# Two moves inside the step of a Mamba-style mixer: where TensorE makes the state products, and which of two VectorE updates goes first

## The chip, the cores and the metric

The kernel runs on one core of one Trainium2 chip. Time is device microseconds (us) of one execution. Five engines run their own instruction lists side by side and meet only at semaphores: TensorE (PE in the profile, its weight loads PEld), VectorE (DVE), ScalarE (ACT), GpSimd (POOL) and SyncE (SP), which here only issues DMA transfers.

## The reference: what is computed

Two batches of 512 tokens, 512 features. Four residual blocks: a block-sparse linear layer, a feed-forward block with 4-bit style dequantised weights, a state-space mixer (Mamba-2 form), and the same feed-forward block again. The change lies in the mixer:

```python
gate, hBC, dt = split(norm(x) @ in_proj_w.T)          # 8192 gate, 8192 x + 2*1024 B,C, 128 dt
x, Bm, Cm = split(silu(causal_conv4(hBC)))            # 128 heads of 64; B, C: 8 groups of 128
M       = (C B^T) * exp(segment_sum(A dt))            # per chunk of 128 tokens: "decayed group product"
Y_diag  = M @ (x dt)                                  # inside a chunk
states  = B_decay^T @ (x dt)                          # what a chunk adds to the state
new     = carry of the states over the chunks         # s[c] = exp(A_last) s[c-1] + states[c]
Y_off   = C @ s * exp(A_cumsum)                       # from earlier chunks
y = rmsnorm(Y_diag + Y_off + D x) * norm_w * silu(gate)
out = y @ out_proj_w.T                                # 8192 -> 512
```

## The kernel before

The mixer is written out as 128 steps `k` (K), each for one batch and one pair of heads (128 channels, all 512 tokens of that batch, 4 chunks of 128), plus five steps that drain it. Each engine has its own order, written by hand, in a loop `for k in range(STEPS)`. There is no planner: the order in the file is the order in each engine's queue.

In step k **TensorE** does: `project` of the x unit k+1 (12 matmuls of 512 columns, L847), `outputs(k-1)` (Y_diag and Y_off of the pair before, L910 and L916), `arguments(k)` (the decay exponents, L873), `turn_x(k)` (four transposes, L885), in every eighth step `gram` (C B^T and B transposed, L857 and L863), `project` of the z (gate) unit k+1, `states(k)` (six small products, L896), in two of eight steps `project` of a b or c unit for the next group, and `project_out`, one tile of the output projection (12 matmuls, L929). The out tiles start at k = 5, the b and c units come at k = 3, 4, 11, 12, and so on, for the groups 1 to 15; gram comes in the step behind the c unit's. Below, these three are called the b step, the c step and the gram step, and the five others ordinary steps.

**VectorE** in step k: `y_low(k-2)` (L1252), `accumulate` of the out tile of step k-1 (L1262), `decay_c(k)` (L1225, the tile ce), the convolution of the x unit k+1 (three instructions, L1171), `scale_x(k)` (x_dec L1193, x_dt L1198), `mask_gram` (L1178) in a gram step, `gate(k-1)` (L1242, L1246), `carry(k)` (a copy L1207 and four small instructions L1213: the state over the chunks), `mask_em(k)` (L1233: the decayed group product em), and behind these the convolution of a b or c unit (L1171 with the tile bc).

**ScalarE** taps a projected bank (`tap`, L1037: first term of the convolution), copies weights (L1025, L1081), does the exponentials (L1063, L1065), `y_high` (L1075), `square` (L1069), the activations of x, z (L1042, L1047), the tap of b or c, and after the c unit's convolution `activate_bc` (L1052). **GpSimd** makes the low parts of the weights (L1350, L1355) and sums squares (L1365).

What ties them: every projected unit, gram, B transposed and out tile goes to one of three PSUM banks (`ring`) in turn, and `ring_free` waits for the reader of the bank three uses earlier. In a gram step the z unit takes the bank of the x unit k+1 of the same step, so it waits for that unit's convolution (`conv_done`). `states(k)` waits for x_dec (`xdec_done`); `carry(k)` for `states(k)` (`st_mm`); `outputs(k)` for em, x_dt, ce and the carried state (`em_done`, `xdt_done`, `ce_done`, `st_done`).

Of the kernel before, what the change touches and what calls it, by code (L numbers as in the profile page):

```python
# [37 lines left out]
K = B * JP  # L38
# [9 lines left out]
def build(nc, x_in, mask_t, wa_t, bias_a, w_in, conv_w, conv_b, dt_bias, a_log, d_res, norm_w, w_out,  # L48
          gu_w, gu_z, gu_s, dn_w, dn_z, dn_s, x_mid, e_t, a_parts, out):
    with ExitStack() as ctx:  # L50
# [644 lines left out]
        def need(eng, s, n):  # L695
            if n > 0:
                eng.wait_ge(s, n)
# [37 lines left out]
        def gram_in(k):  # L735

            if k < 0:
                return [0]
            n, q = k // QG + 1, k % QG
            return [n] if q == 5 and n < NG else []  # L740
# [14 lines left out]
        def ring_bank(banked):  # L755
            return RING[RINGED[banked] % 3]
# [15 lines left out]
        with nc.Block() as block:  # L772
# [52 lines left out]
            def _(pe):  # L825
                def ring_free(banked):
                    at = RINGED[banked] - 3
                    if at < 0:
                        return
                    kind, i = RING_AT[at]  # L830
                    if kind in ("x", "b", "c"):
                        pe.wait_ge(conv_done, CONVED[kind, i] + 1)
                    elif kind == "z":
                        pe.wait_ge(silu_z, i + 1)
                    elif kind == "gram":
                        pe.wait_ge(gt_done, i + 1)
                    elif kind == "btok":
                        pe.wait_ge(btok_done, i + 1)
                    else:
                        pe.wait_ge(acc_done, CPB * i[0] + i[1] + 1)  # L840

                def project(unit):
                    u, b, dst = UNIT[unit], unit_batch(unit), ring_bank(unit)
                    ring_free(unit)
                    pe.wait_ge(w_lo, u + 1)
                    for i, (k, (wp, xp)) in enumerate((k, ab) for k in range(KT) for ab in PASSES):
                        mm = nc.tensor.matmul(dst[:], w_sb[:, u % WR, wp, k * P:(k + 1) * P],  # L847
                                              lnt[:, xp, k, b * S:(b + 1) * S],
                                              start=(i == 0), stop=(i == 3 * KT - 1))
                    mm.then_inc(prj_mm, 1)  # L850
# [38 lines left out]
                def states(k):  # L889
                    pe.wait_ge(xdec_done, k + 1)  # L890
                    pe.wait_ge(btok_done, k // QG + 1)
                    if k == 0:
                        pe.wait_ge(last_done, B)
                    need(pe, st_done, k)
                    for c in range(OFFC):
                        mm = nc.tensor.matmul(ST[:, c * PAIR:(c + 1) * PAIR],  # L896
                                              b_tok[:, k // QG % 2, c * NS:(c + 1) * NS],
                                              x_dec[:, c * PAIR:(c + 1) * PAIR], start=True, stop=True)
                    mm.then_inc(st_mm, 1)

                def outputs(k):
                    pe.wait_ge(em_done, k + 1)
                    pe.wait_ge(xdt_done, k + 1)
                    pe.wait_ge(ce_done, k + 1)
                    pe.wait_ge(st_done, k + 1)
                    need(pe, y_done, k)
                    for c in range(CPB):
                        for h in range(2):
                            at = (2 * c + h) * HD
                            mm = nc.tensor.matmul(YT[h * HD:(h + 1) * HD, c * CS:(c + 1) * CS],  # L910
                                                  x_dt[:, at:at + HD], em[:, h, c * CS:(c + 1) * CS],
                                                  start=True, stop=(c == 0))
                        if c == 0:
                            continue
                        for h in range(2):
                            mm = nc.tensor.matmul(YT[h * HD:(h + 1) * HD, c * CS:(c + 1) * CS],  # L916
                                                  state[:, c - 1, h * HD:(h + 1) * HD],
                                                  ce[:, k % 2, h, (c - 1) * CS:c * CS],
                                                  start=False, stop=True)
                    mm.then_inc(yt_mm, 1)  # L920

                def project_out(i, t):
                    dst = ring_bank(("out", (i, t)))
                    ring_free(("out", (i, t)))
                    pe.wait_ge(yg_lo, HALF * (i + 1))
                    pe.wait_ge(wo_lo, HALF * (i + 1))
                    for m, (j, (yp, wp)) in enumerate((j, ab) for j in range(HALF * i, HALF * (i + 1))
                                                      for ab in PASSES):
                        mm = nc.tensor.matmul(dst[:], ygs[:, j % OR, yp, t * P:(t + 1) * P], wo[:, j % WOR, wp],  # L929
                                              start=(m == 0), stop=(m == 3 * HALF - 1))  # L930
                    mm.then_inc(out_mm, 1)
# [68 lines left out]
                for k in range(STEPS):  # L1000
                    if 0 < k < K - 1:
                        project(("x", k + 1))
                    if 1 <= k <= K:
                        outputs(k - 1)
                    if k < K:
                        arguments(k)
                        turn_x(k)
                    for n in gram_in(k):
                        gram(n)
                    if k + 1 < K:  # L1010
                        project(("z", k + 1))
                    if k < K:
                        states(k)
                    for unit in bc_units(k):
                        project(unit)
                    for i, t in out_tiles(k):
                        project_out(i, t)

            @block.scalar
            def _(act):  # L1020
# [139 lines left out]
            def _(dve):  # L1160
# [41 lines left out]
                def carry(k):  # L1202
                    dve.wait_ge(st_mm, k + 1)
                    if k == 0:
                        dve.wait_ge(last_done, B)
                    need(dve, yt_mm, k)
                    nc.vector.tensor_copy(state[:, 0], ST[:, 0:PAIR]).then_inc(st_part, 1)  # L1207
                    for c in range(1, OFFC):
                        dve.wait_ge(st_part, (2 * OFFC - 2) * k + 2 * c - 1)
                        for h in range(2):  # L1210
                            at = 2 * pair(k) + h
                            last = c == OFFC - 1 and h == 1
                            nc.vector.scalar_tensor_tensor(  # L1213
                                out=state[:, c, h * HD:(h + 1) * HD],
                                in0=state[:, c - 1, h * HD:(h + 1) * HD],
                                scalar=e_last[:, batch(k) * CPB + c, at:at + 1],
                                in1=ST[:, c * PAIR + h * HD:c * PAIR + (h + 1) * HD],
                                op0=ALU.mult, op1=ALU.add)\
                                .then_inc(st_done if last else st_part, 1)
# [9 lines left out]
                def mask_em(k):  # L1229
                    dve.wait_ge(exp_done, k + 1)  # L1230
                    dve.wait_ge(gt_done, k // QG + 1)
                    need(dve, yt_mm, k)
                    nc.vector.tensor_tensor(  # L1233
                        em[:], ARG[:],
                        gt[:, k // QG % 2].rearrange("p (o t) -> p o t", o=1).to_broadcast([P, 2, S]),
                        ALU.mult).then_inc(em_done, 1)
# [87 lines left out]
                for k in range(STEPS + 1):  # L1324
                    if 2 <= k <= K + 1:
                        y_low(k - 2)
                    for i, t in out_tiles(k - 1):
                        accumulate(i, t)
                    if k < K:
                        decay_c(k)  # L1330
                    if k + 1 < K:
                        conv(("x", k + 1))
                    if k < K:
                        scale_x(k)
                    for n in gram_in(k):
                        mask_gram(n)
                    if 1 <= k <= K:
                        gate(k - 1)
                    if k < K:
                        carry(k)  # L1340
                        mask_em(k)
                    for unit in bc_units(k):
                        conv(unit)

# [185 lines left out]
```

## Time and profile before

| | us |
|---|---|
| median of 3 runs (2245.4 to 2248.91) | 2247.79 |
| the profiled execution | 2245.92 |
| its span | 2244.2 |
| PE busy in the span | 2123.8 (95%) |
| DVE busy | 1645.7 (73%) |
| ACT busy | 1389.9 (62%) |
| POOL busy | 891.8 (40%) |

The mixer's steps run from about 355 to 1955 us of the span. In the timeline a row is a run of like instructions: start in us, length in us, engine, line, operation, tile written and tiles read, shape, count; in brackets the idle time of that engine before it and what ended the idle time. Starts are the numbers to go by: ends overlap the next row's start, because the engines are pipelined.

### The profile page before, as it was taken

What the parts mean: (1) busy time and instruction counts of PE and PEld (TensorE: products, weight loads), DVE (VectorE), ACT (ScalarE), POOL (GpSimd) and SP (SyncE); (2) the same over time, 40 slices, a digit from 0 to 9 for tenths busy, and PEclk for the clock granted to TensorE, in tenths of its full rate; (3) what the DMA queues carried; (4) which work ended last, traced back from release to release, by engine and by line L of the source; (5) the groups of instructions that cost most, each with busy time, mean ns of one, the idle gap of its engine ahead of it and who ended that gap; (6) DMA issues with size and microseconds to landing.
All of it is one profiled execution on the core that took longest, in us unless ns stands there. A gap on an engine that the chain in (4) does not pass through costs nothing. (4 is left out here: it accounts for less than half of the span.)

```text
span 2244.2 us, 37403 instructions
## 1 busy us (share of the span) xinstructions
PE 2123.8 (95%) x13374; PEld 1739.7 (78%) x13374; DVE 1645.7 (73%) x2683; ACT 1389.9 (62%) x1872; POOL 891.8 (40%) x637
## 2 busy tenths in 40 slices
PE   5999977899999999999999999999999999959999
PEld 4788865787887878787888888787887878748887
DVE  8655466778787787878787777778787877755554
ACT  2222236777777777777777777777787777622221
POOL 2222123454444445453444445454444444342221
PEclk9999988999999999999999999999999999979999
DMA  4434313333333333333333323333333333323441
GB/s 164 143 128 150 103 63 104 105 98 102 100 101 102 106 95 103 100 97 103 100 104 99 107 96 112 91 107 96 96 107 96 107 96 108 121 92 134 168 134 73
DMA packets 128564, 241.89 MB, mean 108 GB/s; under 512 B 13968, under 2 KB 48528, under 8 KB 128144
## 3 DMA queue, kind: packets, MB, share of 16 engines
q1 hardware_dynamic: 128400, 239.73, 33.3%
q8 instruction: 100, 1.64, 0.3%
q14 instruction: 64, 0.52, 0.1%
HBM read 234.17 MB, written 5.51 MB: 107 GB/s over the span
## 5 line engine op out<-in xcount | busy, mean ns | idle before, releaser
L847 PE MATMUL ring<-m_lnt,w_sb 128*128 128x512 f32 x3456 | 850.0, 395 | 17.7 <-DVE xc L1171 17.7
L847 PEld LDWEIGHTS ring<-m_lnt,w_sb 128*128 128x128 f32 x3456 | 638.6, 189 | 148.4 <-DVE xc L1171 21.4
L1350 POOL TENSOR_TENSOR w_sb<-w_raw,w_sb 128x512 fp32r<-128x512 f32 x288 | 420.0, 1463 | 338.2 <-ACT w_sb L1025 337.4
L1171 DVE SCALAR_TENSOR_TENSOR xc<-ring,cw,xc 128x511 f32<-128x511 f32 (+2 forms) x384 | 287.2, 748 | 183.8 <-ACT xc L1037 174.7
L929 PE MATMUL ring<-wo,ygs 128*128 128x512 f32 x1536 | 383.0, 398 | 2.5 <-POOL wo L1355 2.5
L1365 POOL TENSOR_TENSOR ysq<-ysq,y 128x512 f32<-128x512 f32 x126 | 163.6, 1298 | 542.9 <-ACT y L1069 542.9
L929 PEld LDWEIGHTS ring<-wo,ygs 128*128 128x128 f32 x1536 | 282.5, 189 | 60.6 <-issue 3.1
L1025 ACT ACTIVATE w_sb<-w_raw 128x512 fp32r<-128x512 f32 x288 | 177.4, 622 | 33.4 <-DMA w_raw<-w_in 33.3
L910 PE MATMUL yt<-em,x_dt 128*64 128x128 f32 x2048 | 183.6, 279 | 1.4 <-DVE em L1233 1.4
L1037 ACT ACTIVATE xc<-ring,cb,cw 128x512 f32<-128x512 f32 x128 | 99.2, 775 | 137.4 <-PE ring L847 137.4
L1063 ACT ACTIVATE arg<-arg 128x1024 f32<-128x1024 f32 x128 | 129.0, 1008 | 69.2 <-PE arg L873 69.2
L1355 POOL TENSOR_TENSOR wo<-wo_raw,wo 128x512 fp32r<-128x512 f32 x128 | 170.2, 1329 | 3.3 <-ACT wo L1081 3.3
L365 PE MATMUL bank_e<-f_lnt,f_gu 128*128 128x512 f32 x672 | 159.6, 399 | 11.2 <-DVE f_lnt L135 6.5
L288 POOL TENSOR_TENSOR f_gu<-f_gu_f,f_gu 128x1024 fp32r<-128x1024 f32 x28 | 67.2, 2401 | 251.1 <-ACT f_gu L312 251.1
L1065 ACT ACT_TABLE_LOAD x128 | 164.2, 1283 | 2.3
L1042 ACT ACT_TABLE_LOAD x127 | 162.9, 1283 | 2.3
L365 PEld LDWEIGHTS bank_e<-f_lnt,f_gu 128*128 128x128 f32 x672 | 129.9, 194 | 39.7 <-issue 10.6
L365 PE MATMUL bank<-f_lnt,f_gu 128*128 128x512 f32 x672 | 154.1, 390 | 3.5 <-DVE f_hf L251 1.8
L1233 DVE TENSOR_TENSOR em<-arg,gt 128x1024 f32<-128x1024 f32 x128 | 155.8, 1217 | 0.1
L910 PEld LDWEIGHTS yt<-em,x_dt 128*64 128x64 f32 x2048 | 118.0, 136 | 46.7 <-issue 43.3
L365 PEld LDWEIGHTS bank<-f_lnt,f_gu 128*128 128x128 f32 x672 | 125.9, 188 | 30.3 <-issue 4.1
L916 PE MATMUL yt<-ce,state 128*64 128x128 f32 x1536 | 149.1, 273 | 0.0
(176 smaller groups left out, 3081.4 us busy)
## 6 DMA issues: line engine op xcount, KB each, us to landing
w_raw<-w_in SPq DMA_DIRECT2D x288, 256.0 KB, 4.3
ce<-e_t SPq DMA_DIRECT2D x128, 384.0 KB, 4.2
wo_raw<-w_out SPq DMA_DIRECT2D x128, 256.0 KB, 4.5
f_gu_q<-gu_w SPq DMA_DIRECT2D x28, 512.0 KB, 5.2
f_gu_zr<-gu_z SPq DMA_DIRECT2D x28, 512.0 KB, 6.8
f_gu_sr<-gu_s SPq DMA_DIRECT2D x28, 512.0 KB, 8.0
f_dn_q<-dn_w SPq DMA_DIRECT2D x28, 256.0 KB, 7.1
f_dn_zr<-dn_z SPq DMA_DIRECT2D x28, 256.0 KB, 7.8
```

The lines of the kernel that those rows point to most:

```text
L365: mm = nc.tensor.matmul(dst[half][:], gu[:, j, b, c:c + P], lnt[:, a, k, half * TOK:(half + 1) * TOK], start=(i == 0), stop=(i == 3 * KT - 1))
L847: mm = nc.tensor.matmul(dst[:], w_sb[:, u % WR, wp, k * P:(k + 1) * P], lnt[:, xp, k, b * S:(b + 1) * S], start=(i == 0), stop=(i == 3 * K ...
L910: mm = nc.tensor.matmul(YT[h * HD:(h + 1) * HD, c * CS:(c + 1) * CS], x_dt[:, at:at + HD], em[:, h, c * CS:(c + 1) * CS], start=True, stop ...
L929: mm = nc.tensor.matmul(dst[:], ygs[:, j % OR, yp, t * P:(t + 1) * P], wo[:, j % WOR, wp], start=(m == 0), stop=(m == 3 * HALF - 1))
L1025: nc.scalar.activation(w_sb[:, u % WR, 0], w_raw[:, u % NR], ACT.Copy).then_inc(w_hi, 1)
L1042: nc.scalar.activation(xc[:, k % 3], xc[:, k % 3], ACT.Silu).then_inc(silu_x, 1)
L1065: nc.scalar.activation(part, part, ACT.Exp, scale=-1.0).then_inc(exp_done, 1)
L1171: nc.vector.scalar_tensor_tensor(out=dst[:, d:S], in0=src[:, 0:S - d], scalar=cw[:, tile, j:j + 1], in1=dst[:, d:S], op0=ALU.mult, op1=ALU ...
L1233: nc.vector.tensor_tensor(em[:], ARG[:], gt[:, k // QG % 2].rearrange("p (o t) -> p o t", o=1).to_broadcast([P, 2, S]), ALU.mult).then_inc ...
L1350: nc.gpsimd.tensor_tensor(w_sb[:, u % WR, 1], w_raw[:, u % NR], w_sb[:, u % WR, 0].bitcast(F32), ALU.subtract).then_inc(w_lo, 1)
L1355: nc.gpsimd.tensor_tensor(wo[:, j % WOR, 1], wo_raw[:, j % 2], wo[:, j % WOR, 0].bitcast(F32), ALU.subtract).then_inc(wo_lo, 1)
L1365: nc.gpsimd.tensor_tensor(part, part, y[:, k % 2], ALU.add).then_inc(ysq_done, 1)
```

## The change

On TensorE `states(k)` goes behind the b or c unit and the out tile, to the end of the step. On VectorE `mask_em(k)` goes ahead of `carry(k)`. Nothing is added or taken away.

```diff
--- before.py
+++ after.py
@@ -1009,12 +1009,12 @@
                         gram(n)
                     if k + 1 < K:
                         project(("z", k + 1))
-                    if k < K:
-                        states(k)
                     for unit in bc_units(k):
                         project(unit)
                     for i, t in out_tiles(k):
                         project_out(i, t)
+                    if k < K:
+                        states(k)
 
             @block.scalar
             def _(act):
@@ -1337,8 +1337,8 @@
                     if 1 <= k <= K:
                         gate(k - 1)
                     if k < K:
+                        mask_em(k)
                         carry(k)
-                        mask_em(k)
                     for unit in bc_units(k):
                         conv(unit)
```

## Rows read from the trace of the kernel before

**Rows 1.** The page, part 1: busy time of each engine in the span.
```profile
PE 2123.8 (95%) x13374; PEld 1739.7 (78%) x13374; DVE 1645.7 (73%) x2683; ACT 1389.9 (62%) x1872; POOL 891.8 (40%) x637
```

**Rows 2.** Waits, 350 to 1900 us: total us, times, longest.
```profile
DVE state L1207 <- PE st L896: 47.9, 106, 4.3
...
PE ring L847 <- DVE xc L1171: 17.7, 16, 3.4
...
PE st L896 <- DVE x_dec L1193: 15.6, 14, 3.6
```

**Rows 3.** Timeline of PE, an ordinary step: states, out tile, next x unit.
```profile
1041.57 0.83 PE L896 MATMUL st<-x_dec,b_tok 128*128 128x128 f32 x6
1042.15 3.02 PE L929 MATMUL ring<-wo,ygs 128*128 128x512 f32 x12
1045.01 2.88 PE L847 MATMUL ring<-m_lnt,w_sb 128*128 128x512 f32 x12
```

**Rows 4.** Timeline of DVE, the same step.
```profile
1042.43 0.29 DVE L1207 COPY state<-st 128x128 f32<-128x128 f32 x1 [0.37 <-PE st L896]
...
1043.66 1.22 DVE L1233 TENSOR_TENSOR em<-arg,gt 128x1024 f32<-128x1024 f32 x1
...
1048.74 2.31 DVE L1171 SCALAR_TENSOR_TENSOR xc<-ring,cw,xc 128x511 f32<-128x511 f32 x3 [1.80 <-ACT xc L1037]
```

**Rows 5.** Timeline of PE, from the x unit ahead of a c step to the gram step.
```profile
1004.23 2.88 PE L847 MATMUL ring<-m_lnt,w_sb 128*128 128x512 f32 x12
...
1013.38 0.94 PE L896 MATMUL st<-x_dec,b_tok 128*128 128x128 f32 x6 [0.94 <-DVE x_dec L1193]
...
1019.63 2.88 PE L847 MATMUL ring<-m_lnt,w_sb 128*128 128x512 f32 x12
...
1027.20 3.03 PE L847 MATMUL ring<-m_lnt,w_sb 128*128 128x512 f32 x12 [0.88 <-DVE xc L1171]
```

**Rows 6.** Timeline of DVE, the same stretch.
```profile
1004.50 2.32 DVE L1171 SCALAR_TENSOR_TENSOR bc<-ring,cw,bc 128x511 f32<-128x511 f32 x3 [3.13 <-ACT bc L1037]
...
1008.75 1.88 DVE L1225 TENSOR_TENSOR ce<-ce,bc 128x768 f32<-128x768 f32 x1
1010.55 2.31 DVE L1171 SCALAR_TENSOR_TENSOR xc<-ring,cw,xc 128x511 f32<-128x511 f32 x3
...
1019.68 2.31 DVE L1171 SCALAR_TENSOR_TENSOR bc<-ring,cw,bc 128x511 f32<-128x511 f32 x3 [1.97 <-ACT bc L1037]
```

**Rows 7.** Timeline of ACT, the same stretch.
```profile
1018.88 0.77 ACT L1037 ACTIVATE bc<-ring,cb,cw 128x512 f32<-128x512 f32 x1
1022.03 1.06 ACT L1052 ACTIVATE bc<-bc 128x1024 f32<-128x1024 f32 x1 [2.38 <-DVE bc L1171]
```

**Rows 8.** Timeline of POOL, the same stretch.
```profile
1008.54 1.27 POOL L1350 TENSOR_TENSOR w_sb<-w_raw,w_sb 128x512 fp32r<-128x512 f32 x1 [0.86 <-ACT w_sb L1025]
```

**Rows 9.** Timeline of PE, two groups later: a c step without a wait.
```profile
1206.12 2.88 PE L847 MATMUL ring<-m_lnt,w_sb 128*128 128x512 f32 x12
...
1220.33 2.88 PE L847 MATMUL ring<-m_lnt,w_sb 128*128 128x512 f32 x12
...
1227.86 3.02 PE L847 MATMUL ring<-m_lnt,w_sb 128*128 128x512 f32 x12 [0.84 <-DVE xc L1171]
```

**Rows 10.** Timeline of PE, steps 126 and 127, with no x unit between.
```profile
1938.81 0.83 PE L896 MATMUL st<-x_dec,b_tok 128*128 128x128 f32 x6
1939.39 3.02 PE L929 MATMUL ring<-wo,ygs 128*128 128x512 f32 x12
1942.34 0.66 PE L910 MATMUL yt<-em,x_dt 128*64 128x128 f32 x8
```

**Rows 11.** Timeline of PE at two idle times of over 2 us.
```profile
326.48 0.65 PE L955 MATMUL xt<-ident,dt_h 128*128 128x128 f32 x4 [2.28 <-DVE dt_h L1297]
...
1957.27 12.75 PE L929 MATMUL ring<-wo,ygs 128*128 128x512 f32 x48 [2.54 <-POOL wo L1355]
```

**Rows 12.** Windows behind those: length, busy PE to POOL, granted PEclk, DMA, GB/s.
```profile
326.40:327.50 1.10, 1.02 (x9) 1.03 (x10) 0.35 (x2) 0.00 (x0) 0.00 (x0) 1.00 0.01 2
...
1957.20:1958.00 0.80, 0.73 (x2) 0.66 (x3) 0.00 (x0) 0.00 (x0) 0.00 (x0) 0.53 0.63 241
```

## The prediction

> **What bounds the kernel now.** I read the busy line first: TensorE is busy for 95% of the span and VectorE for 73% [rows 1]. So the question is only where TensorE idles in the mixer, and whether the change touches it. The list of waits answers that for 350 to 1900 us: 15.6 us in 14 waits of the state products for x_dec, and 17.7 us in 16 waits of a projection for the convolution xc [rows 2]. All of TensorE's other time there is matmuls. The 47.9 us that VectorE waits for the state products [rows 2] are idle time of an engine that is not the bound.
>
> The timeline then says where the two waits stand. In an ordinary step there is none: states, out tile and next x unit follow each other [rows 3]. They come once per group of eight steps: 0.94 us ahead of states in the c step, 0.88 us ahead of the z unit in the gram step [rows 5]. Both have one source, a chain VectorE -> ScalarE -> VectorE through these three steps: the convolution of the b unit (1004.50), ce (1008.75), the convolution of the x unit (1010.55), x_dec and the gate behind it [rows 6], ScalarE's tap of the c unit (1018.88), the convolution of the c unit (1019.68), ScalarE's activation of B and C (1022.03) [rows 6, 7] and, after it in ScalarE's queue, the tap of the next x unit, that unit's convolution, and then the z unit at 1027.20 [rows 5]. The most the change can win is the first wait, about 15 us in all, if the second does not grow by as much.
>
> **TensorE, ordinary steps.** The same work in another order: z, out, states, x instead of z, states, out, x. States take 1042.15 - 1041.57 = 0.58 us, the out tile 1045.01 - 1042.15 = 2.86 us [rows 3]; the sum stays. States now start 0.58 us ahead of the next x unit, here at 1044.43. The carry can start 1042.43 - 1041.57 = 0.86 us after states start [rows 3, 4] and frees VectorE 1043.66 - 1042.43 = 1.23 us later [rows 4], so 2.09 us after states start: 1046.52. `outputs` needs the carried state behind the x unit, at 1045.01 + 2.8 = 1047.8. It is ready 1.3 us early. No wait, cost nothing; the cover is the x unit.
>
> **VectorE, ordinary steps.** em moves ahead, into the time in which VectorE now waits for states. The carry ends at 1046.52. Behind it are queued y_low, accumulate and ce, which take about 2.15 us (they filled the time from the end of em, about 1044.8, to the start of the 1.80 us wait, 1046.94 [rows 4]). 1046.52 + 2.15 = 1048.67, and the next convolution started at 1048.74, waiting for its tap [rows 4]. It just fits. The 0.37 and 1.80 us of idle time per step become one wait of about 2.2 us in front of the carry.
>
> What may be late next is ce. One row shows ce at 1.88 us, started at 1008.75 while GpSimd's subtraction ran from 1008.54 to 1009.81 [rows 6, 8]; VectorE went on only 0.74 us after GpSimd had ended. In ordinary steps ce and y_low now fall 1.7 us later, onto GpSimd's two subtractions. So the convolution may be late by up to one such hold, about 1.3 us, in some steps. I price this at nothing, as it is absorbed by the 2.2 us wait in front of the carry of the same step. Bounds: nothing, and (if two holds come together) 2.6 - 2.2 = 0.4 us in each of some 75 ordinary steps, 30 us. I take nothing, since the row shows one hold.
>
> The Trainium skill, page "SBUF — State Buffer", in its part on the port pair that VectorE and GpSimd share, has the rule: an exclusive lock, and a VectorE operation with two SBUF inputs is blocked for the whole of a GpSimd instruction that started first, and the other way round. The trace agrees (1.88 us beside 1.27 us of GpSimd). By that rule a VectorE instruction can be held anew by each GpSimd instruction, and both y_low and ce have two SBUF inputs; this is the rule that speaks against the change, and the rival on holds below is its result.
>
> **The b, c and gram steps.** Count from the x unit that stands ahead of the c step, T0 = 1004.23 [rows 5].
> - b step: states now come at T0 - 0.58, the carry frees VectorE at T0 + 1.51 = 1005.74. The convolution of the b unit, queued behind the carry, started at 1004.50: 1.24 us later. But then y_low, at about 1007.98, falls into GpSimd's idle time (0.86 us up to 1008.54 [rows 8]) and is not held, and ce meets the same instruction of GpSimd (1008.54 to 1009.81, which follows TensorE, not VectorE) and ends where it did: the x convolution stays at 1010.55. Cost nothing, cover: the time ce was held anyway. If that cover is gone, up to 1.24 us.
> - c step: the wait of 0.94 us goes, since states now stand 5.5 us later, far behind x_dec. A c step without the wait is in the trace: from x unit to x unit 1220.33 - 1206.12 = 14.21 us [rows 9], against 1019.63 - 1004.23 = 15.40 [rows 5]. TensorE gets 1.19 us ahead.
> - what is late next: the convolution of the c unit is queued behind the carry. States start at T0 + 14.21 - 0.58 = T0 + 13.63, VectorE is free at T0 + 13.63 + 2.09 = T0 + 15.72. Before, this convolution started at 1019.68 = T0 + 15.45, released by ScalarE's tap. So the moved states set it, 0.27 us later than before.
> - gram step: from that convolution to the z unit the chain has no slack: 1027.20 - 1019.68 = 7.52 us [rows 5, 6]. The z unit comes at T0 + 15.72 + 7.52 = T0 + 23.24, against T0 + 22.97 before. TensorE, 1.19 us ahead, waits 0.88 + 1.19 + 0.27 = 2.34 us there. The saved wait is handed back whole, with 0.27 us on top.
>
> Fifteen groups have these steps. In twelve the rows are as above: 12 x 0.27 = 3.2 us. In two (z unit at 1227.86 and about 100 us later) TensorE had no wait in the c step, because the chain ran faster: from T0 to z 1227.86 - 1206.12 = 21.74 us [rows 9]. There the carry is the new limit, and z comes at T0 + 23.24: 2 x 1.50 = 3.0 us. In the first group ScalarE's chain sets both ends, and I take nothing.
>
> **The end.** In steps 126 to 127 no x unit follows. outputs(126) started 2.95 us after the out tile [rows 10]. Now the out tile starts at 1938.81, states about 2.8 us later at 1941.6, the carry is done at 1941.6 + 2.09 = 1943.7, and outputs(126) starts then instead of at 1942.34: 1.4 us. In step 127 the same happens again, with VectorE already late by it; together 1.5 us, between 1.0 and 2.0. Nothing hides this: the tail waits for outputs(127).
>
> **Sum.** 3.2 + 3.0 + 1.5 = 7.7 us. On the profiled execution: 2245.9 + 7.7 = 2253.6 us. That execution lies 1.9 us under the median of the runs, 2247.8, so for a median I forecast 2247.8 + 7.7, about 2255 us (+0.3%). Changes under 0.2%, 4.5 us, can't be told from none.
>
> **Rivals.**
> - **The clock falls.** Behind an idle time of 2.28 us the granted clock was 1.00; behind one of 2.54 us it was 0.53, half speed (1.2 instead of 2.4 GHz) [rows 11, 12]. The new wait in the gram step, 2.34 us, lies between. Where it fell, 48 matmuls took 12.75 us [rows 11]; four runs of 12 take 4 x 2.73 = 10.9 in full clock (a run of 12 behind another), so it costs 1.8 us a time. In all 14 groups 26 us: 2281 us; in half of them 2268 us. For it: 2.34 is over the longest idle time that is shown harmless. Against: by 0.06 us only. Chance 0.2.
> - **Holds make VectorE the bound** in ordinary steps: y_low and ce both held, 2.6 us against 2.2 us of wait, up to 30 us, 2285 us at most. Against: VectorE's idle time hardly runs out with one hold. Chance 0.04.
> - **Faster: the first wait goes and the second does not take it.** Place: the c step. It would decide if the convolution of the c unit started at least 0.5 us earlier than T0 + 15.45, that is, if carry and tap were both early: then 0.94 us of 12 to 14 groups stay won, less the end's 1.5 us: -11 us, 2237 us. For it: the two short groups, where that chain is 1.23 us shorter. Against: carry needs states, and states stand at T0 + 13.63 by TensorE's own pace. Chance 0.10.
> - **Nothing to be seen:** the 0.27 us is not there (the carry comes in time) and only the two short groups and the end cost: 3 to 4.5 us, 2251 us. Chance 0.16.
>
> **Numbers.** Forecast 0.50. In a fifth of it the result falls under 4.5 us. Slower: 0.40 + 0.20 + 0.04 = 0.64. Same: 0.10 + 0.16 = 0.26. Faster: 0.10. The range goes from 2247 (the null case with the scatter of the runs, 3.5 us) to 2272 (the clock lost in more than half of the groups).
>
> **What would show it.** In the waits: states for x_dec gone; the projection's wait for xc up from 17.7 us to about 35 us in 16 waits of 2.2 to 2.4 us; VectorE's wait for st up from 48 us to over 200 us, and its wait for the tap of xc nearly gone. In the timeline: the convolution of the c unit directly behind the carry, not behind a tap; T0 to z in the gram step 23.2 us in all fifteen groups but the first; outputs(126) behind a wait for the carry (or st). Wrong if T0 to z is under 22.9 us, if waits for the state appear ahead of outputs in ordinary steps, or if the granted clock is under 1 behind the gram step.

## The result, and the profile after

| | before | changed |
|---|---|---|
| median, 6 runs each, us | 2246.86 (2244.93 to 2248.91) | 2254.89 (2253.13 to 2259.19) |
| profiled execution, us | 2245.92 | 2253.62 |
| its span, us | 2244.2 | 2251.9 |

The ratio is 1.004, 95% interval 1.0027 to 1.0052: slower by about 8 us, clear of the 0.2% that can be told.

The waits in the same window as [rows 2] (engine and line, who was waited for, total us, times, longest):

```profile
DVE state L1207 <- PE st L896: 229.5, 118, 4.2
...
PE ring L847 <- DVE xc L1171: 26.4, 16, 3.4
...
PE ring L847 <- ACT sz L1047: 6.7, 14, 0.5
...
PE yt L910 <- DVE state L1213: 2.3, 3, 0.9
...
PE st L896 <- DVE x_dec L1193: 1.2, 1, 1.2
```

TensorE's wait for x_dec has all but gone (15.6 to 1.2 us), its wait for xc has grown (17.7 to 26.4 us), and a new one is there, 14 times about 0.5 us: an x unit waits for ScalarE's activation of z to free its bank. VectorE's wait for the products has grown from 47.9 to 229.5 us, and costs nothing by itself.

TensorE, from the x unit ahead of a c step to the gram step, the stretch of [rows 5]:

```profile
1006.07 0.83 PE L896 MATMUL st<-x_dec,b_tok 128*128 128x128 f32 x6
1006.66 3.02 PE L847 MATMUL ring<-m_lnt,w_sb 128*128 128x512 f32 x12
...
1020.29 0.83 PE L896 MATMUL st<-x_dec,b_tok 128*128 128x128 f32 x6
1021.58 3.06 PE L847 MATMUL ring<-m_lnt,w_sb 128*128 128x512 f32 x12 [0.46 <-ACT sz L1047]
...
1029.89 3.04 PE L847 MATMUL ring<-m_lnt,w_sb 128*128 128x512 f32 x12 [1.44 <-DVE xc L1171]
```

VectorE in the same stretch, against [rows 6]:

```profile
1011.59 1.59 DVE L1225 TENSOR_TENSOR ce<-ce,bc 128x768 f32<-128x768 f32 x1
1013.10 2.31 DVE L1171 SCALAR_TENSOR_TENSOR xc<-ring,cw,xc 128x511 f32<-128x511 f32 x3
...
1021.15 0.29 DVE L1207 COPY state<-st 128x128 f32<-128x128 f32 x1 [2.11 <-PE st L896]
1021.48 0.98 DVE L1213 SCALAR_TENSOR_TENSOR state<-state,e_last,st 128x64 f32<-128x64 f32 x4
1022.38 2.31 DVE L1171 SCALAR_TENSOR_TENSOR bc<-ring,cw,bc 128x511 f32<-128x511 f32 x3
```

The convolution of the c unit starts directly behind the carry, at T0 + 15.72 (1022.38 - 1006.66), and z in the gram step at T0 + 23.23 (1029.89 - 1006.66).

Where the 7.7 us of span came from, by the starts of TensorE's landmarks: from the z unit of the first gram step to that of the second 100.94 us before, 102.98 after (+2.04); the 13 further intervals to the last gram step 1309.98 before, 1314.01 after (+4.03: before, 11 of about 100.96 and 2 of about 99.72 us; after, all of about 101.08); from there to the square sums 138.58 before, 140.51 after (+1.93); the rest -0.3. In the first group TensorE waits twice, 2.51 us ahead of gram and 2.57 us ahead of the z unit, and runs the z unit at half clock. Its rows, and three windows (length, busy PE to POOL, PEclk, DMA, GB/s):

```profile
417.47 1.16 PE L857 MATMUL ring<-bc 128*128 128x128 f32 x8 [2.51 <-ACT bc L1052]
...
421.53 4.93 PE L847 MATMUL ring<-m_lnt,w_sb 128*128 128x512 f32 x12 [2.57 <-DVE xc L1171]
```
```profile
418.00:418.80 0.80, 0.80 (x9) 0.72 (x7) 0.00 (x0) 0.80 (x2) 0.79 (x1) 1.00 0.01 5
418.90:419.00 0.10, 0.06 (x1) 0.00 (x0) 0.00 (x0) 0.10 (x1) 0.10 (x1) 0.50 0.00 0
421.50:423.00 1.50, 1.47 (x4) 1.20 (x5) 1.50 (x3) 1.49 (x3) 0.23 (x1) 0.50 0.04 11
```

The clock is at 0.50 already at 418.90 us, ahead of the second wait (421.53 - 2.57 = 418.96): it fell behind the first, the wait of gram for ScalarE's activation. The kernel before has no such wait there. Its z unit, behind a wait of 2.05 us, runs at full clock, and the next row starts 2.88 us later; here that is 4.76 us.

### The profile page after: what moved, and what is told of

The parts are those of the page before. It is cut to its first block and busy times, and to the rows that moved or that the text cites. A ratio compares the mean times of both kernels' runs of the same rounds, so it can differ in the third digit from the quotient of the medians.

```text
span 2251.9 us, 37403 instructions
## 1 busy us (share of the span) xinstructions
PE 2127.8 (94%) x13374; PEld 1745.5 (78%) x13374; DVE 1680.3 (75%) x2683; ACT 1389.9 (62%) x1872; POOL 926.3 (41%) x637
## 5 line engine op out<-in xcount | busy, mean ns | idle before, releaser
L847 PE MATMUL ring<-m_lnt,w_sb 128*128 128x512 f32 x3456 | 860.0, 399 | 33.1 <-DVE xc L1171 26.4
L1350 POOL TENSOR_TENSOR w_sb<-w_raw,w_sb 128x512 fp32r<-128x512 f32 x288 | 410.9, 1431 | 335.7 <-ACT w_sb L1025 335.3
L929 PE MATMUL ring<-wo,ygs 128*128 128x512 f32 x1536 | 369.0, 389 | 2.4 <-POOL wo L1355 2.4
L929 PEld LDWEIGHTS ring<-wo,ygs 128*128 128x128 f32 x1536 | 288.3, 188 | 62.8 <-issue 3.1
L1355 POOL TENSOR_TENSOR wo<-wo_raw,wo 128x512 fp32r<-128x512 f32 x128 | 215.7, 1685 | 3.3 <-ACT wo L1081 3.3
L1207 DVE COPY state<-st 128x128 f32<-128x128 f32 x128 | 37.3, 292 | 238.3 <-PE st L896 238.3
L1225 DVE TENSOR_TENSOR ce<-ce,bc 128x768 f32<-128x768 f32 x128 | 183.8, 1436 | 0.0
L1075 ACT ACTIVATE ygs<-sz 128x512 fp32r<-128x512 f32 x128 | 80.9, 632 | 128.4 <-DVE sz L1246 128.4
```

The costliest lines, as they stand in the source:

```text
L1225: nc.vector.tensor_tensor(ce[:, k % 2], ce[:, k % 2], c_off.rearrange("p (o t) -> p o t", o=1) .to_broadcast([P, 2, OFFC * CS]), ALU.mult) ...
L1350: nc.gpsimd.tensor_tensor(w_sb[:, u % WR, 1], w_raw[:, u % NR], w_sb[:, u % WR, 0].bitcast(F32), ALU.subtract).then_inc(w_lo, 1)
L1355: nc.gpsimd.tensor_tensor(wo[:, j % WOR, 1], wo_raw[:, j % 2], wo[:, j % WOR, 0].bitcast(F32), ALU.subtract).then_inc(wo_lo, 1)
```

## The experiments

My theory was the prediction's: the loss is the carry, which waits for products that TensorE makes at T0 + 13.6 us, and which stands ahead of the c unit's convolution in VectorE's queue. The rivals: VectorE's new order by itself; the holds between VectorE and GpSimd; TensorE's order by itself. Medians are of 4 to 8 runs; each ratio is against the kernel before on the same chip.

### One half at a time

Only em ahead of the carry:

```diff
-                        carry(k)
                         mask_em(k)
+                        carry(k)
```

> Only VectorE's half of the change: em ahead of the carry, the state products where they were. Theory (the loss comes from the carry standing behind state products that come at T0 + 13.6 us): no change, 2244 to 2249 us, T0 to z of the gram step still 22.97 us, because the products come early and em and carry fill the same time in either order. Rival (the loss comes from VectorE's own new order, em ahead of the carry): slower by most of the 8 us, 2252 us or more.

Measured: 2233.57 us, ratio 0.9945 (0.9932 to 0.9959). Neither: 12 to 14 us **faster**. Half of the change was a gain, and I had priced it at nothing. The reason is in the c step. VectorE and GpSimd of this kernel:

```profile
1001.91 0.67 DVE L1262 TENSOR_TENSOR xr<-xr,ring 128x512 f32<-128x512 f32 x1
1002.51 0.95 DVE L1225 TENSOR_TENSOR ce<-ce,bc 128x768 f32<-128x768 f32 x1
1003.38 2.30 DVE L1171 SCALAR_TENSOR_TENSOR xc<-ring,cw,xc 128x511 f32<-128x511 f32 x3
```
```profile
1002.65 1.96 POOL L1350 TENSOR_TENSOR w_sb<-w_raw,w_sb 128x512 fp32r<-128x512 f32 x1 [1.21 <-ACT w_sb L1025]
```

ce starts at 1002.51, 0.14 us ahead of GpSimd's subtraction. It takes 0.95 us and GpSimd is held (1.96 us); before, GpSimd came first and ce took 1.88 us [rows 6, 8]. So these two engines meet not only at semaphores. TensorE of the same kernel:

```profile
998.35 2.88 PE L847 MATMUL ring<-m_lnt,w_sb 128*128 128x512 f32 x12
...
1012.56 2.88 PE L847 MATMUL ring<-m_lnt,w_sb 128*128 128x512 f32 x12
...
1020.02 3.02 PE L847 MATMUL ring<-m_lnt,w_sb 128*128 128x512 f32 x12 [0.77 <-DVE xc L1171]
```

T0 to z is 21.67 us, not 22.97: this group now looks like the two short ones of before [rows 9]. The traces show that the start order decides it. In the kernel before, ce starts 0.05 and 0.07 us ahead of GpSimd in the two short groups, and 0.03 to 0.21 us behind it in the twelve others. With em first it is ahead by 0.02 to 0.22 us in 13 of 14 groups; in the one where it is behind, T0 to z is 22.95 us. VectorE's ce and GpSimd's subtraction, first in a short group of the kernel before, then in that one group of this kernel:

```profile
1210.34 0.94 DVE L1225 TENSOR_TENSOR ce<-ce,bc 128x768 f32<-128x768 f32 x1
...
1210.42 2.02 POOL L1350 TENSOR_TENSOR w_sb<-w_raw,w_sb 128x512 fp32r<-128x512 f32 x1 [1.14 <-ACT w_sb L1025]
```
```profile
1401.49 1.27 POOL L1350 TENSOR_TENSOR w_sb<-w_raw,w_sb 128x512 fp32r<-128x512 f32 x1 [0.87 <-ACT w_sb L1025]
...
1401.69 1.89 DVE L1225 TENSOR_TENSOR ce<-ce,bc 128x768 f32<-128x768 f32 x1
```

Eleven groups that turn short, at 1.25 us each, are 13.8 us, which is the whole gain from the first gram step to the last (1397.1 against 1410.9 us). What brought ce forward is small. In ordinary steps em starts in the 0.37 us in which VectorE waited for the products; ce follows earlier and holds up GpSimd's subtraction for the b unit less (two subtractions in 2.88 us, 3.06 before), the buffer's next transfer lands sooner (ScalarE waits 1.86 us for it, 2.22 before), and the tap of the b unit comes sooner. That each of these links passes the time on is read from the rows, not tested one by one.

Only the state products last:

```diff
-                    if k < K:
-                        states(k)
                     for unit in bc_units(k):
                         project(unit)
                     for i, t in out_tiles(k):
                         project_out(i, t)
+                    if k < K:
+                        states(k)
```

> Only TensorE's half: the state products last, the carry still ahead of em. Theory: in the c step VectorE waits for the products with em still behind the carry, so the c unit's convolution starts 1.14 us later than in the changed kernel, T0 + 16.9, and z of the gram step at T0 + 24.4: 14 groups x 1.14 = 16 us more than the changed kernel, 2271 us, and TensorE's wait for xc up to 45 us or more. In ordinary steps em ends about 0.2 us ahead of outputs, so waits may appear there too, up to 0.5 us x 75, then 2300 us. Rival (TensorE's order alone costs the 8 us and em's place nothing): 2255 us.

Measured: 2285.9 us, ratio 1.017 (1.0156 to 1.0183). TensorE's half costs 38 us alone and 21 us once em is out of the way (2233.6 to 2254.9). It lies between the two guesses, 2271 and 2300. The first guess's reason is there in full: T0 to z is 24.36 us (1018.08 to 1042.44), 24.4 expected, 1.13 more than in the changed kernel. The second's is not. The waits, and the starts of `outputs` in two ordinary steps:

```profile
PEld yt L910 <- DVE em L1233: 33.6, 91, 1.1
...
PE ring L847 <- ACT sz L1047: 21.2, 23, 1.4
...
PE yt L910 <- DVE em L1233: 1.4, 2, 0.7
```
```profile
971.09 0.66 PE L910 MATMUL yt<-em,x_dt 128*64 128x128 f32 x8
...
982.58 0.66 PE L910 MATMUL yt<-em,x_dt 128*64 128x128 f32 x8
```

In 91 steps the weight loads of `outputs` (PEld) wait for em, which stands behind the late carry, but the matmuls lose nothing by it: an ordinary step takes 11.49 us from `outputs` to `outputs` here, in the changed kernel and in the kernel before. What comes on top of T0 to z are waits for z's activation, now also of the x unit at T0 (in 9 of 14 groups, 0.2 to 1.3 us), and the clock. Behind the wait ahead of the gram step's z unit the twelve matmuls take over 4 us instead of 3.0 in 4 of the 14 groups behind the first, as here:

```profile
1042.44 4.61 PE L847 MATMUL ring<-m_lnt,w_sb 128*128 128x512 f32 x12 [1.86 <-DVE xc L1171]
```

### Where the products stand

The products behind the b or c unit, but ahead of the out tile, em first:

```diff
                     for unit in bc_units(k):
                         project(unit)
+                    if k < K:
+                        states(k)
                     for i, t in out_tiles(k):
                         project_out(i, t)
-                    if k < K:
-                        states(k)
```

> The state products behind the b or c unit but ahead of the out tile; em ahead of the carry. Differs from before on TensorE in 30 of 128 steps only. Theory: TensorE's wait for x_dec in the c step is gone as in the changed kernel, but the carry is done at about T0 + 13, ahead of the tap, so the c unit's convolution goes back to T0 + 15.45 and z to T0 + 22.97; the end is as before. So the saved wait is handed back whole and nothing is lost: 2244 to 2249 us, as before, with the wait in the gram step at about 2 us. Rival (the saved 0.9 us per c step is worth its time once the carry is early): 2234 us. Rival (moved products cost wherever they go): 2252 us.

Measured: 2236.05 us, ratio 0.9953 (0.9939 to 0.9966), level with em first alone (2233.57). So the place behind the c unit neither gains nor costs; what costs (19 us from here to the changed kernel) is the 2.7 us more, behind the out tile, that put the carry past the tap. The gain is em's, not the moved products': T0 to z is 1021.38 - 999.69 = 21.69 us here, and it ends with the same wait, 0.78 us. I had this kernel "as before" because I did not know what em first does; the statement that the saved wait is handed back stands, against em first.

The changed kernel with the c (and b) unit's convolution ahead of the carry:

```diff
                     if k < K:
                         mask_em(k)
-                        carry(k)
                     for unit in bc_units(k):
                         conv(unit)
+                    if k < K:
+                        carry(k)
```

> The changed kernel with one edit: on VectorE the convolution of the b or c unit goes ahead of the carry. Theory: the c unit's convolution is set by the tap again, T0 + 15.4 instead of T0 + 15.72, z of the gram step at T0 + 22.97 instead of 23.23; outputs waits for the carry in b and c steps instead, which the chain covers. 14 x 0.26 = 3.6 us off: 2251 us, still over before by the end's and the first group's 4 us. Rival (the carry is not what holds the convolution, holds by GpSimd are): z stays at T0 + 23.2 and the time at 2255 us. If the new waits of outputs are not covered, about 1 us x 30 on top, 2285 us.

Measured: 2267.11 us, ratio 1.0085 (1.0071 to 1.0099), slower than the changed kernel by 12 us. `outputs` now waits for the carry, 1.25 and 0.92 us in the b and c steps, and that is not covered, as I had put it as the third case; T0 to z grows to 24.08 us (1011.22 to 1035.30). The carry can stand ahead of the convolution or behind it: at T0 + 13.6 us the products are too late for either.

### The chain in the c step

The kernel before, with ce out of the chain:

```diff
-                    if k < K:
-                        decay_c(k)
                     if k + 1 < K:
                         conv(("x", k + 1))
...
                         gate(k - 1)
                     if k < K:
+                        decay_c(k)
                         carry(k)
                         mask_em(k)
```

> The kernel before with ce (decay_c) moved on VectorE from ahead of the x convolution to behind the gate; nothing else. Theory (the chain through the c step is as long as it is because ce stands in it and is held by GpSimd): the x convolution starts about 1.8 us earlier there, x_dec and the tap of the c unit with it, both waits of TensorE go: about 2 us x 12 groups and 1 us x 2, 2220 to 2225 us. Rival (ce would be overlapped anyway and the gain of em first came from the shorter waits for st): within 3 us of before.

Measured: 2217.22 us, ratio 0.9871 (0.9856 to 0.9886). As the theory had it, from rows of the kernel before alone. TensorE has no idle time left in the middle of the mixer (window of 1400 us, same columns as above):

```profile
440.00:1840.00 1400.00, 1400.00 (x9823) 1157.10 (x9822) 1111.26 (x1916) 1095.10 (x1448) 613.65 (x483) 1.00 0.33 103
```

GpSimd is busy for 613.65 us there, 649.60 before: ce and GpSimd's subtractions no longer meet as often.

Moving ce takes away its own 0.95 us from this chain as well as the hold, so this run alone does not part the two.

The same edit on the changed kernel:

> The changed kernel with the same move of ce. Theory: there the carry, behind state products at T0 + 13.6, sets the c unit's convolution, T0 + 15.72, whatever the x convolution does, so z of the gram step stays at T0 + 23.2 and the time at 2252 to 2257 us; only the wait of the x unit for the gate's activation (0.46 us) goes, into the wait for xc. Rival (holds on ce are what makes the changed kernel slow): 2235 us or less.

Measured: 2270.82 us, ratio 1.0107 (1.0091 to 1.0122): 16 us over the changed kernel, where I had expected nothing. T0 to z is 23.24 us (1009.64 to 1032.88), so the theory of the carry holds to 0.01 us although ce is never held here (its longest is 0.95 us). The time is lost in another way. Two of the fourteen gram steps behind the first group's, and the window behind the first of the two:

```profile
1032.88 4.61 PE L847 MATMUL ring<-m_lnt,w_sb 128*128 128x512 f32 x12 [2.20 <-DVE xc L1171]
...
1443.56 3.01 PE L847 MATMUL ring<-m_lnt,w_sb 128*128 128x512 f32 x12 [2.19 <-DVE xc L1171]
```
```profile
1034.80:1037.00 2.20, 2.20 (x6) 1.74 (x6) 2.17 (x4) 1.04 (x2) 0.00 (x0) 0.50 0.21 78
```

In 12 of 14 groups the z unit takes about 4.6 us instead of 3.0 and the clock is at 0.50 (1.2 GHz); in two it stays up. 12 x 1.6 = 19 us; the first gram step's z unit comes 3.2 us earlier than in the changed kernel (418.34 against 421.53), and the rest is the size of the loss. ce's removal took away the x unit's wait for z's activation, so that the idle time became one piece of 2.19 us. In the changed kernel it comes in two, about 0.5 and 1.44 us, with matmuls between them, and the clock stays up in these 14 groups. The clock rival of the prediction was real, and the changed kernel escaped it by what I had not seen. Whether the split or the shorter second piece saved it is not shown: in the kernel with only the products last, two pieces of about 1.2 and 1.8 us lost the clock in 4 of 14 groups.

The changed kernel with the tap of the x unit ahead of two weight copies on ScalarE, in gram steps:

```diff
+                    early_tap = bool(gram_in(k))
+                    if early_tap:
+                        tap(("x", k + 1))
                     for unit in ahead[0:1]:
                         w_high(unit)
                     for j in wo_of(k):
                         wo_high(j)
-                    if 0 < k < K - 1:
+                    if 0 < k < K - 1 and not early_tap:
                         tap(("x", k + 1))
```

> The changed kernel with the tap of the x unit ahead of the two weight copies on ScalarE, in gram steps. Theory (in the changed kernel too the gram step's z unit is the end of the chain carry, c convolution, activation, tap, x convolution): z comes 0.77 us earlier, VectorE's wait for that tap goes, TensorE's wait for xc falls from 1.4 to 0.7 us: 14 x 0.77 = 11 us less, 2244 us, level with before. Rival (the state products themselves or the holds cost the time): 2252 us or more.

Measured: 2242.19 us, ratio 0.9971 (0.9961 to 0.9982) to a before of 2248.49 us. As expected: z comes at T0 + 22.38 (1004.73 to 1027.11), the wait for xc is 0.55 us instead of 1.44.

The same edit on em first:

> em ahead of the carry alone, 2234 us, plus one edit on ScalarE: in gram steps the tap of the x unit goes ahead of the two weight copies. Theory (the remaining 0.77 to 0.86 us wait per gram step is the end of the same chain): the tap comes 1.0 us earlier, VectorE can use 0.77 us of it, so the wait falls to under 0.1 us: 14 x 0.77 = 11 us less, 2223 us. Rival (the weight copies, later by 0.7 us, hold up a projection instead): 2234 us or more.

Measured: 2219.42 us, ratio 0.9884 (0.9869 to 0.9899): 14 us under em first alone. The direction is the theory's, the size 3 us more than I had worked out. From the first gram step to the last it is 10.5 us (1386.6 against 1397.1), close to the 11 expected. Of the rest, 1.3 us are at the end, where the last 48 matmuls take 11.17 us, not 12.51: the clock stayed up there in this run. And 1.6 us are in the first group, whose z unit comes at 420.20 instead of 421.83 us, a group that I had left out of the sum.

### The end

```diff
+                    if K - 2 <= k < K:
+                        states(k)
                     for unit in bc_units(k):
                         project(unit)
                     for i, t in out_tiles(k):
                         project_out(i, t)
-                    if k < K:
+                    if k < K - 2:
                         states(k)
```

> The changed kernel, but in the last two steps, 126 and 127, the state products in their old place ahead of the out tile. Theory: the waits of 1.60 and 2.10 us ahead of outputs go and the stretch from the last gram step's z unit to the square sums is as before, 138.6 instead of 140.5 us: 1.9 us less, 2253 us. Rival (the end costs nothing): 2255 us. The difference is at the edge of what the runs can tell; the trace decides.

Measured: 2254.13 us, ratio 1.0035 (1.0021 to 1.0049), beside 2254.89 for the changed kernel in another set of runs. The times can't tell. In the trace the stretch from the last gram step's z unit to the square sums is 139.21 us, against 140.51 in the changed kernel and 138.58 before: 1.3 us back, not 1.9. The wait of 1.60 us has gone, but that ahead of `outputs(127)` is still 1.17 us, for the carry, where the kernel before has one of 0.72 for em. The clock falls at the last out tiles again, as in the kernel before (12.77 and 12.75 us for 48 matmuls). In the changed kernel it is at `outputs(127)` that it falls:

```profile
1949.96 0.66 PE L910 MATMUL yt<-em,x_dt 128*64 128x128 f32 x8 [1.60 <-DVE state L1213]
...
1958.14 1.07 PE L910 MATMUL yt<-em,x_dt 128*64 128x128 f32 x8 [2.10 <-DVE state L1213]
...
1966.82 11.16 PE L929 MATMUL ring<-wo,ygs 128*128 128x512 f32 x48 [2.36 <-POOL wo L1355]
```

Up to the last 48 matmuls the changed kernel loses 3.5 us: its two waits are 3.70 us where the kernel before has 1.37, and the half clock costs about 1.6. The last 48 matmuls, 12.75 us before behind an idle time of 2.54 us [rows 11], take 11.16 us behind one of 2.36, so 1.6 us come back.

### The best version

TensorE's order of before; em ahead of the carry, ce behind the gate, and the early tap:

> The best of what the runs point to, with TensorE's order of before: em ahead of the carry, ce behind the gate, the tap of the x unit first in gram steps. Theory: ce behind the gate alone (2217 us) has already removed both waits of TensorE between the first group and the end, so the other two edits have nothing left to win: 2215 to 2219 us. Rival (the three gains add up, 13 + 29 + 14 us): 2195 us or less.

Measured: 2213.21 us, ratio 0.9843 (0.983 to 0.9857), the fastest of all. That is 2 us under the expected range. The three gains don't add up, as expected: TensorE is busy for all of the 1400 us from 440 to 1840. Beside ce alone the medians are 4 us apart, the profiled spans 6.1 us. Of these 5.2 lie in the first group: z starts 3.6 us earlier there, and behind it the clock is up, behind a wait of 0.93 us, where with ce alone it is at half behind one of 2.00:

```profile
416.36 3.01 PE L847 MATMUL ring<-m_lnt,w_sb 128*128 128x512 f32 x12 [0.93 <-DVE xc L1174]
```
```profile
419.98 4.61 PE L847 MATMUL ring<-m_lnt,w_sb 128*128 128x512 f32 x12 [2.00 <-DVE xc L1171]
```

The first row is the best version's, the second that of ce alone.

## Why the prediction was right, point by point

- **The sum.** 7.7 us forecast, 7.7 us of span and 8.0 us of medians measured. That is closer than the terms deserve: the twelve groups came out 1.8 us under their term and the first group 1.9 us over its own, and that these cancel is luck.
- **The handed-back wait and the carry as the new limit**: right, T0 + 15.72 and T0 + 23.24 forecast, T0 + 15.72 and T0 + 23.23 measured. Shown as a cause by the late ce on the changed kernel, which leaves T0 to z at 23.24, and by the products ahead of the out tile, which bring it back.
- **The twelve groups**: 3.2 us forecast, 1.4 us measured (12 x 0.12). The chain was right and the mark was not. T0, the start of an x unit, now stands behind the state products, and from there to `outputs` it takes 2.95 us (1036.07 to 1039.02) instead of 2.81 (1045.01 to 1047.82 before). So T0 itself comes 0.14 us earlier against the work around it: from z to the next T0 TensorE needs 0.12 us less (77.86 against 77.98), and the 0.27 us behind T0 shrink to about 0.13 in all. That a whole step stays as long was right, 11.49 us. The two short groups: 3.0 forecast, 2.7 measured, for the same reason.
- **The first group**: priced at nothing, cost 1.9 us. The end of the chain was where I put it (z at 421.53, 421.57 before), but the clock fell behind a new wait of 2.51 us ahead of gram, and z's matmuls ran at 0.50. The wait of 2.57 us is not needed for it: with the products ahead of the out tile, and with the early tap, the same 2.51 us stand ahead of gram, only 1.49 and 0.30 us ahead of z, and z still takes over 4.2 us. The prediction named a clock under 1 behind the gram step as a sign of being wrong; it came, in this one group.
- **The end**: 1.5 forecast, 1.9 measured. The waits alone account for that (about 2 us more than before); a clock loss and a clock gain of about 1.6 us each, which I had not in it, cancelled by luck.
- **The b step's cover**: right. ce was still held by GpSimd's instruction (1.59 us), the x convolution started at T0 + 6.44, 6.32 before.
- **Ordinary steps at nothing**: right; they take 11.49 us in both kernels. ce is held in most of them (its median is 1456 ns, 951 before), y_low in one of five, and the wait in front of the carry takes it up. The waits for the state ahead of `outputs`, another sign of being wrong, are three, 2.3 us in all, all ahead of the first gram step.
- **What I missed**: the x unit's wait for z's activation, 14 times, which split the idle time of 2.34 us (2.19 in one piece with ce late, less by the 0.14 above), so that the wait for xc is 26.4 us and not about 35; and the worth of em first. For the change as a whole I did not need it, because the late carry overrides it, so the time came out right. But that em only moves ahead into idle time, and so is worth nothing, is wrong as a statement on that edit: alone it is worth 13 us. My own row showed the two short groups in which ce won against GpSimd, by 1.23 us each, and I took their shortness as given instead of asking what would make all groups so.

## What to carry to other kernels

A wait on the bounding engine is worth its time only if the chain that ends it is not the same that ends the next wait; price the chain from a fixed mark to the last of its waits, not the first wait. Of an order change with several parts, price each alone as well as together: here one half won 13 us, the other lost 21. When idle time of about 2 us is gathered into one piece, look at the clock behind it before counting on the sum of waits. And when a group of rows is shorter than its like, find out which row came first there: here two short groups of fourteen showed what em first alone would win in eleven more.

## What the runs showed of the hardware

- The clock of TensorE fell to 0.50 in 12 of 14 equal places behind an idle time of 2.19 us, and stayed at 1.00 in two; elsewhere it stayed up behind 2.28 us [rows 11, 12]. With the products last alone it fell behind 1.86 us and stayed up behind 2.48 (z unit at 1765.05). So the length of one idle time does not decide alone. The price was 1.6 us for twelve matmuls of 512 columns (4.61 instead of 3.01 us).
- Which of VectorE's ce and GpSimd's subtraction starts first decides which is held, and the one behind lost about 0.7 to 1.1 us (1.96 instead of 1.27 us; 1.88, at most 2.06, instead of 0.95). In the c steps of the kernel before, of em first, of the products in the middle and of em with the early tap, 56 in all, leads of 0.01 to 0.25 us one way and 0.03 to 0.21 us the other went with it without exception; with the convolution ahead there is one place, in the first group, where GpSimd's row starts 0.03 us earlier and is the one held, so at such a lead the rows do not tell. It recurs in every group, which is how an edit that moves VectorE by a third of a microsecond is worth 13 us. The Trainium skill, page "SBUF — State Buffer", section "SBUF: two separate sides", has this exclusive hold of the shared port pair for the whole instruction of whichever starts first; the traces here agree to about 0.13 us (ce starts 0.21 us behind a subtraction of 1.27 us: 1.06 + 0.95 = 2.01 us by that rule, 1.88 measured).
